# Padding rows sent one behind each of eight loads per queue, and a POOL wait for the copies of one tile only

## The chip, the cores and the metric

The kernel runs on one core of a Trainium2 chip. The metric is the device time of one execution in microseconds (us), lower is better. The engines are PE (TensorE), DVE (VectorE), ACT (ScalarE), POOL (GpSimd) and SP (SyncE); each works through its own list of instructions in order, and they wait for one another through semaphores (counters). SP and POOL issue DMAs here.

## What is computed

An attention layer (with batch normalisation of q, k and v), a layer norm, and then a mixture of eight experts of which every token uses the best two, followed by a second layer norm. There are 32 x 256 = 8192 tokens of 128 numbers, and an expert has 512 hidden units. The part that matters here, cut from the reference:

```python
        logits = _ln(xf, router_ln_scale, router_ln_bias) @ router_w.T + router_b
        probs = jax.nn.softmax(logits, axis=-1)
        topw, topi = jax.lax.top_k(probs, K)
        topw = topw / jnp.sum(topw, axis=-1, keepdims=True)
        gates = jnp.zeros((T, E), xf.dtype).at[jnp.arange(T)[:, None], topi].set(topw)

        def expert(ls, lb, W1, B1, W2, B2):
            h = jax.nn.gelu(_ln(xf, ls, lb) @ W1.T + B1, approximate=False)
            return h @ W2.T + B2
        ys = jax.vmap(expert)(expert_ln_scale, expert_ln_bias, w1, b1, w2, b2)
        out = jnp.einsum('te,etd->td', gates, ys)
    x = _layernorm(x + _L0_attn_ref(x, ...), axis=-1)
    x = _layernorm(x + _L0_ffn_ref(x, ...), axis=-1)
```

## The kernel before

**Stages.** After the set-up, 32 batches go through the attention (up to about 143 us). For each batch POOL scatters its tokens' rows by their first choice of expert into queue1, a table in device memory in which each expert has a region of its own (`scatter`, L551). Then comes the expert stage, in two passes over tiles of 128 rows. Pass 1 has N1 = 71 tiles, 0 to 70: it loads 128 rows of queue1, runs the first choice's expert on them, and POOL scatters the result by the second choice into queue2. Pass 2 has tiles 71 to 141: it loads 128 rows of queue2, runs the second expert, adds and normalises, and POOL scatters the rows into the output. The first NTILE0 = 29 tiles of a pass are listed early, from the counts of the first 18 batches; the other 42 are listed later, once all rows are counted.

**Padding.** An expert's region ends anywhere, but a tile takes 128 rows. So behind the end of each of the eight regions of either queue 128 padding rows are written: sixteen DMAs, which SP issues (`pad`, L417: the end is read from `ends_i`, then one DMA from SBUF to the queue). DVE writes `ends_i` in `list_second_group` (L1362) and raises `s_pad`; POOL raises `s_pad2` when the rows for the second queue carry their numbers. Tiles 29 to 70 of pass 1 may take in padding rows of queue1, tiles 100 to 141 of pass 2 those of queue2.

**SP's order.** SP issues the load of tile j into slot j % 16 (`load_rows`, L423), which first waits for `s_yo` of that slot: the rows of tile j - 16 have been sent and have landed. Up to here SP does 29 loads, then the sixteen pads, then waits for all of the pads, then loads on. Between the two passes it waits for the sends of the tiles that the next loads need (`rows_written`, L432).

**The loop of a tile.** PE transposes a tile's rows (L847), multiplies by the first weights (L854, eight matmuls in the view, 128 x 128 each) and, one tile later, by the second (L864). DVE normalises the rows (L1406, waits for the load), adds the bias (L1400) and adds the result to the rows (`first_result`, L1428, raises `s_ac`). In pass 2 DVE ends a tile with `finish` (L1452), which waits for POOL's root.

**POOL's order.** In pass 1 one turn is `carry(j + 2)`, two small operations on one column of 128 numbers (L568, L569) that put a tile's numbers into its outgoing rows, and `send_on(j)` (L572), the scatter of tile j (L577). `send_on` waits for `s_ac` and, by `pg.settle()` without an argument, until every copy that POOL has issued so far is complete, those of tile j + 2 too. `settle(at)` waits for a count of its own copies (L54). In pass 2 a turn is `root(j)` (L584) and `send_out(j - 1)` (L590).

Of the kernel before, what the change touches and what calls it, by code (L numbers as in the profile page):

```python
# [58 lines left out]
def wait(eng, sem, value):  # L59

    if isinstance(value, int) and value <= 0:
        return
    eng.wait_ge(sem, value)
# [25 lines left out]
def build(nc, x, x_t, wide, low, r_b, w1_t, b1_rows, w2_t, b2, out):  # L89
    NB, T, C = x.shape  # L90
    _, E, H = w1_t.shape
    R = low.shape[0]
    HC = H // P
# [9 lines left out]
    NTILE0 = NB0 * TPB - (E - 1)  # L103

    N1 = NT + E - 1
# [24 lines left out]
    with ExitStack() as ctx:  # L130
# [3 lines left out]
        def sem(name):  # L134
            return ctx.enter_context(nc.semaphore(name))
# [127 lines left out]
        def fold_bank(e):  # L263
# [63 lines left out]
        s_n0, s_tot, s_tabp, s_tabt, s_tab, s_pad, s_zero, s_n0t = [sem(n) for n in (  # L327
            "s_n0", "s_tot", "s_tabp", "s_tabt", "s_tab", "s_pad", "s_zero", "s_n0t")]
        s_rows, s_pad2 = [sem(n) for n in ("s_rows", "s_pad2")]
# [13 lines left out]
        s_padd = sem("s_padd")  # L343
# [28 lines left out]
        def own_wait(eng, s_own):  # L372


            eng.sem_inc(s_own, 1)
# [15 lines left out]
        @block.sync  # L391
        def _(sp):

            def load_chunk(c):
                sp.dma_start(x_all[:, c * CH:(c + 1) * CH, DATA:DATA + P], x_chunks[c]).then_inc(s_x[c], 16)

            def load_columns(c):
                here = slice(c * XT_B * T, (c + 1) * XT_B * T)
                sp.dma_start(xT[:, here], x_t[:, here]).then_inc(s_xt[c], 16)

            for c in range(NCH):
                load_chunk(c)
            for e in range(E):
                sp.dma_start(w1r[:, e], w1_t[:, e]).then_inc(s_w1[e // 3], 16)
                if e + 1 in (W1_FIRST, E - 2):
                    load_columns(int(e >= W1_FIRST))
            for c in range(2, NB // XT_B):
                load_columns(c)
            for e in range(E):
                sp.dma_start(w2T[:, e], w2_t[:, e]).then_inc(s_w2, 16)  # L410
            sp.dma_start(b2_bc[:], b2.rearrange("e d -> (e d)").partition_broadcast(P)).then_inc(s_go, 16)

            sp.wait_ge(s_rows, 1)
            sp.dma_start(queue1[DUMMY:DUMMY + E * P, :].rearrange("(a p) c -> p a c", p=P), pad_rows[:]).then_inc(s_zero, 16)
            sp.dma_start(queue2[DUMMY:DUMMY + E * P, :].rearrange("(a p) c -> p a c", p=P), pad2_rows[:]).then_inc(s_zero, 16)

            def pad(e, second):  # L417
                n = E + e if second else e
                end = sp.value_load(ends_i[0:1, n:n + 1], min_val=e * CAP, max_val=e * CAP + NTOK)
                rows = (pad2_rows if second else pad_rows)[:, e, :]  # L420
                sp.dma_start((queue2 if second else queue1)[bass.ds(end, P), :], rows).then_inc(s_padd, 16)

            def load_rows(j):  # L423
                slot = j % XR
                wait(sp, s_yo[slot], j // XR * 16)
                row = sp.value_load(tab_row[0:1, j:j + 1], min_val=0, max_val=DUMMY + (E - 1) * P)
                if j < N1:
                    sp.dma_start(xg[:, slot, 0:W1], queue1[bass.ds(row, P), :]).then_inc(s_xg[slot], 16)
                else:
                    sp.dma_start(xg[:, slot, :], queue2[bass.ds(row, P), :]).then_inc(s_xg[slot], 16)  # L430

            def rows_written(n_tiles):  # L432

                for j in range(n_tiles - XR, n_tiles):
                    sp.wait_ge(s_yo[j % XR], 16 * (j // XR + 1))

            sp.wait_ge(s_scat[0], SCAT * NB0)
            sp.wait_ge(s_tab, 1)
            for j in range(NTILE0):
                load_rows(j)  # L440
            sp.wait_ge(s_pad, 1)
            sp.wait_ge(s_pad2, 1)
            for second in (False, True):
                for e in range(E):
                    pad(e, second)
            sp.wait_ge(s_scat[1], SCAT * (NB - NB0))
            sp.wait_ge(s_padd, 16 * 2 * E)
            sp.wait_ge(s_tab, 2)
            for j in range(NTILE0, N1):
                load_rows(j)  # L450
            rows_written(N_UP)
            for j in range(N1, N1 + NTILE0):
                load_rows(j)
            rows_written(N1)
            for j in range(N1 + NTILE0, NTILE):
                load_rows(j)
            rows_written(NTILE)
# [3 lines left out]
        def _(pool):  # L461
            pg = Progress(pool, s_pool)
# [88 lines left out]
            def scatter(b):  # L551
# [5 lines left out]
                for t in range(TPB):  # L557
# [3 lines left out]
                        out=queue1, out_offset=bass.IndirectOffsetOnAxis(x_int[:, b * TPB + t, POS1:POS1 + 1], 0),  # L561
                        in_=x_all[:, b * TPB + t, DATA:DATA + W1], in_offset=None).then_inc(s_scat[b >= NB0], 16)

            def carry(j):
                slot = j % XR
                pool.wait_ge(s_gm, j + 1)
                sd = xg[:, slot, ROOT0 - DATA:ROOT0 - DATA + 1]
                pg.did(pool.tensor_tensor(orow[:, slot, SQ0:SQ0 + 1], sd, sd, ALU.mult))  # L568
                pg.did(pool.tensor_copy(orow_int[:, slot, TOK2:TOK2 + 1],  # L569
                                        xg_int[:, slot, TOK - DATA:TOK - DATA + 1]))  # L570

            def send_on(j):  # L572
                slot = j % XR
                pool.wait_ge(s_ac, j + 1)
                pg.settle()
                own_wait(pool, s_own_pool)
                pool.indirect_dma_start(  # L577
                    out=queue2, out_offset=bass.IndirectOffsetOnAxis(xg_int[:, slot, POS2 - DATA:POS2 - DATA + 1], 0),
                    in_=orow[:, slot, :], in_offset=None).then_inc(s_yo[slot], 16)
# [18 lines left out]
            for j in range(CARRY_AHEAD):  # L598
                carry(j)
            for j in range(N1):  # L600
                if j + CARRY_AHEAD < N1:
                    carry(j + CARRY_AHEAD)
                send_on(j)
# [939 lines left out]
```

## Time and profile before

| what | value |
|---|---|
| median of 3 runs | 466.83 us (465.84 to 467.15) |
| profiled execution, its time | 464.84 us |
| its span, first to last instruction | 463.0 us |
| PE busy | 414.6 us, 90% |
| ACT busy | 323.5 us, 70% |
| POOL busy | 321.0 us, 69% |
| DVE busy | 285.0 us, 62% |
| mean granted TensorE clock | 0.949 |

Times in the trace are us from the start of the span. The shares are means over stages with different limits, so a stage is read from its own waits and from the pace of its tiles. A matmul's end is modelled; starts are good for pacing. In a timeline a row is a start, a length, the engine, the line and the operation, and in brackets the idle time of the engine ahead of it with what ended that. SPq is SP's own list of instructions. A clock of 1.00 is 2.4 GHz and 0.50 is 1.2 GHz.

### The profile page before, as it was taken

The page shows a single profiled execution, that of the slowest core. Times are in us where ns is not written, and L with a number is a line of the kernel's source. Part 1 is how long each engine was busy: PE and PEld are TensorE (multiplying, and loading weights), DVE is VectorE, ACT ScalarE, POOL GpSimd, SP SyncE. Part 2 cuts the span into 40 slices and gives each one's busy share as a digit, 9 for nine tenths or more (in the row PEclk, how much of TensorE's full clock was granted, in tenths as well). Part 3 has the DMA queues.
Part 4 walks back from the last instruction along what each step waited for, and adds up shares of the span by engine and source line. Part 5 has one row for each costly group of instructions (what it writes and reads, how often), then busy time and mean ns, then how long its engine had stood idle before and what let it go on. Part 6 is the DMA issues. An engine that isn't in the chain of part 4 may idle for free. (4 is left out here: it accounts for less than half of the span.)

```text
span 463.0 us, 14354 instructions
## 1 busy us (share of the span) xinstructions
PE 414.6 (90%) x3464; PEld 395.7 (85%) x3468; DVE 285.0 (62%) x1612; ACT 323.5 (70%) x826; POOL 321.0 (69%) x538
## 2 busy tenths in 40 slices
PE   8989899999985999960999999995999999999970
PEld 7967788999875989960999999994999999999970
DVE  2455967999996575520555555532666667666662
ACT  2137688999886677850688788883788888887830
POOL 7000577999899866666656656566888888688885
PEclk9999999999995899995899999998899999999995
DMA  9999211111124123344443333444333333333210
GB/s 233 332 405 334 61 36 38 44 45 44 38 69 107 44 60 90 100 130 146 120 118 96 90 89 90 120 121 133 104 107 104 105 106 104 100 94 105 71 36 28
DMA packets 45057, 50.90 MB, mean 110 GB/s; under 512 B 6562, under 2 KB 37026, under 8 KB 44978
## 3 DMA queue, kind: packets, MB, share of 16 engines
q1 hardware_dynamic: 36880, 30.67, 24.7%
q0 software_dynamic: 7728, 18.51, 11.9%
q10 hardware_dynamic: 370, 0.80, 0.6%
q8 instruction: 33, 0.54, 0.5%
q14 instruction: 46, 0.38, 0.3%
HBM read 28.23 MB, written 21.72 MB: 108 GB/s over the span
## 5 line engine op out<-in xcount | busy, mean ns | idle before, releaser
L864 PE MATMUL bank<-w2T,xT 128*128 x1136 | 153.5, 279 | 6.2 <-DVE yt L1400 6.2
L854 PE MATMUL bank<-xT 128*128 128x128 f32 x1136 | 155.3, 281 | 2.1 <-issue 2.1
L864 PEld LDWEIGHTS bank<-w2T,xT 128*128 128x128 f32 x1136 | 141.4, 196 | 6.6 <-issue 6.6
L854 PEld LDWEIGHTS bank<-xT 128*128 128x128 f32 x1136 | 142.4, 197 | 2.4 <-issue 2.4
L886 ACT ACTIVATE xT<-w1T,zero_col 128x512 f32 x142 | 102.4, 722 | 42.3 <-issue 39.6
L577 POOL DMA_INDIRECT queue<-xT,xg x71 | 71.4, 1006 | 57.8 <-POOL xT L569 34.7
L1400 DVE TENSOR_TENSOR yt<-bank,b_bc 128x128 f32<-128x128 f32 x142 | 41.4, 291 | 94.4 <-PE bank L864 66.3
L590 POOL DMA_INDIRECT out<-xT,xg x71 | 75.3, 1061 | 17.1 <-issue 17.1
L1007 ACT ACTIVATE xT<-bank 128x512 f32<-128x512 f32 x142 | 82.2, 579 | 4.3 <-PE bank L854 3.5
L886 ACT ACTIVATE xT<-bank,one_col 128x128 f32<-128x128 f32 x142 | 52.1, 367 | 34.6 <-PE bank L847 29.1
L560 POOL DMA_INDIRECT queue<-x_all x64 | 62.3, 973 | 11.5 <-issue 6.9
L544 POOL MEMSET idle<- 128x512 f32 x64 | 34.5, 538 | 27.3 <-ACT x_all L982 26.7
L584 POOL TENSOR_TENSOR r_z<-ve_z,neg_half 128x1 f32<-128x1 f32 x71 | 42.0, 592 | 4.6 <-DVE ve_z L1447 0.5
L1406 DVE TENSOR_SCALAR xT<-xg 128x128 f32<-128x128 f32 x71 | 26.9, 379 | 17.4 <-DMA xg<-queue 17.1
L847 PE MATMUL bank<-ident,xT 128*128 128x128 f32 x71 | 20.7, 291 | 18.5 <-issue 15.1
L1452 DVE TENSOR_SCALAR xT<-zt,mv_z,r_z 128x128 f32<-128x128 f32 x71 | 26.7, 377 | 16.9 <-POOL r_z L584 16.9
L847 PEld LDWEIGHTS bank<-ident,xT 128*128 128x128 f32 x71 | 10.4, 147 | 19.7 <-issue 18.4
L1428 DVE SCALAR_TENSOR_TENSOR xT<-yt,xg 128x128 f32<-128x128 f32 x71 | 25.1, 354 | 0.1
L1434 DVE SCALAR_TENSOR_TENSOR zt<-yt,xg 128x128 f32<-128x128 f32 x71 | 23.9, 336 | 0.0
L713 PE MATMUL bank<-wvvT,xT 128*128 128x144 f32 x128 | 21.1, 288 | 0.0
L1220 DVE SCALAR_TENSOR_TENSOR x_all<-bank,rinv,x_all 128x136 f32<-128x136 f32 x62 | 19.3, 352 | 1.7 <-issue 0.5
L1439 DVE BATCH_NORM_STATS2 st_z<-zt 128x6 f32<-128x128 f32 x71 | 20.1, 283 | 0.0
(232 smaller groups left out, 726.9 us busy)
## 6 DMA issues: line engine op xcount, KB each, us to landing
xg<-queue SPq DMA_DIRECT2D x71, 129.5 KB
xg<-queue SPq DMA_DIRECT2D x71, 67.5 KB
x_all<-x SPq DMA_DIRECT2D x16, 256.0 KB, 6.1
xT<-x_t SPq DMA_DIRECT2D x8, 512.0 KB, 10.4
w1r<-w_t SPq DMA_DIRECT2D x8, 256.0 KB, 6.4
w2T<-w_t SPq DMA_DIRECT2D x8, 256.0 KB, 11.3
queue<-xT,xg POOLq DMA_INDIRECT x71
out<-xT,xg POOLq DMA_INDIRECT x71
```

Of the source, the lines that this page charges most:

```text
L544: pg.did(pool.memset(idle[:, 0:4, :], 0.0))
L560: pool.indirect_dma_start(out=queue1, out_offset=bass.IndirectOffsetOnAxis(x_int[:, b * TPB + t, POS1:POS1 + 1], 0), in_=x_all[:, b * TPB ...
L577: pool.indirect_dma_start(out=queue2, out_offset=bass.IndirectOffsetOnAxis(xg_int[:, slot, POS2 - DATA:POS2 - DATA + 1], 0), in_=orow[:, s ...
L584: pool.tensor_tensor(r_z[:, at], ve_z[:, at], neg_half[:, 0:1], ALU.pow).then_inc(s_pw, 1)
L590: pool.indirect_dma_start(out=out, out_offset=bass.IndirectOffsetOnAxis(xg_int[:, slot, TOK2:TOK2 + 1], 0), in_=orow[:, slot, 0:P], in_off ...
L847: tr(bank[q % 2][:, 0:P], (orow if k < N1 else xg)[:, slot, 0:P], ident[:]).then_inc(s_gt, 1)
L854: last = mm(bank[2 + s][:, h * P:(h + 1) * P], w1c[:, (q - 1) % WR, h * P:(h + 1) * P], xgT[:, s, :], start=True, stop=True)
L864: last = mm(bank[4 + s][:, 0:P], hs[:, s, h, :], w2T[:, bass.ds(e, 1), h, :].rearrange("p a d -> p (a d)"), start=(h == 0), stop=(h == HC ...
L886: return act.activation(out_, in_, ACT.Identity, bias=bias)
L1007: act.activation(hs[:, s].rearrange("p h t -> p (h t)"), bank[2 + s][:], ACT.Gelu).then_inc(s_hs, 1)
L1400: v.tensor_tensor(yt[:, j % 2, :], bank[4 + j % 2][:, 0:P], b2_bc[:, bass.ds(e * P, P)], ALU.add).then_inc(s_ys, 1)
L1406: v.tensor_scalar(orow[:, slot, 0:P], xg[:, slot, 0:P], xg[:, slot, MEAN - DATA:MEAN - DATA + 1], xg[:, slot, ROOT - DATA:ROOT - DATA + 1] ...
```

## The change

SP no longer issues the sixteen pads in a row behind load 28. It issues a pad of queue1 behind each of the loads 21 to 28, and a pad of queue2 behind each of the loads 63 to 70. Each of the first eight waits for `s_pad` and `s_pad2`, which are counters that stay up once raised. Ahead of load 29 SP waits for the eight pads of queue1 alone, and ahead of load 100 for all sixteen. POOL notes in `carried[j]` how many of its copies had been issued when `carry(j)` was done, and `send_on(j)` waits for that many.

```diff
             for j in range(NTILE0):
                 load_rows(j)
-            sp.wait_ge(s_pad, 1)
-            sp.wait_ge(s_pad2, 1)
-            for second in (False, True):
-                for e in range(E):
-                    pad(e, second)
+                if j >= NTILE0 - E:
+                    sp.wait_ge(s_pad, 1)
+                    sp.wait_ge(s_pad2, 1)
+                    pad(j - (NTILE0 - E), False)
             sp.wait_ge(s_scat[1], SCAT * (NB - NB0))
-            sp.wait_ge(s_padd, 16 * 2 * E)
+            sp.wait_ge(s_padd, 16 * E)
             sp.wait_ge(s_tab, 2)
             for j in range(NTILE0, N1):
                 load_rows(j)
+                if j >= N1 - E:
+                    pad(j - (N1 - E), True)
             rows_written(N_UP)
             for j in range(N1, N1 + NTILE0):
                 load_rows(j)
             rows_written(N1)
+            sp.wait_ge(s_padd, 16 * 2 * E)
             for j in range(N1 + NTILE0, NTILE):
                 load_rows(j)
...
+            carried = {}
+
             def carry(j):
...
                 pg.did(pool.tensor_copy(orow_int[:, slot, TOK2:TOK2 + 1],
                                         xg_int[:, slot, TOK - DATA:TOK - DATA + 1]))
+                carried[j] = pg.n
 
             def send_on(j):
                 slot = j % XR
                 pool.wait_ge(s_ac, j + 1)
-                pg.settle()
+                pg.settle(carried[j])
```

On SP, around the loads of tiles 22 and 23 (they wait for `s_yo6` and `s_yo7`), this stands in a row before:

```order
L426 TENSOR_LOAD tab [waits s_yo6]
L426 ISA x2
L428 ISA
L428 DMA xg<-queue 128x135
L426 TENSOR_LOAD tab [waits s_yo7]
L426 ISA x2
L428 ISA
L428 DMA xg<-queue 128x135
```

And in the changed kernel, from the load of tile 22 to that of tile 23:

```order
L426 TENSOR_LOAD tab [waits s_yo6]
L426 ISA x2
L428 ISA
L428 DMA xg<-queue 128x135
L419 TENSOR_LOAD ends_i [waits s_pad2,s_pad]
L419 ISA x2
L421 ISA
L421 DMA queue<-pad_rows 128x135
L426 TENSOR_LOAD tab [waits s_yo7]
```

A pad with its register load has moved in between the two loads.

On SP, at the load of tile 29, the first of the second list, before (the last of the sixteen pads goes to queue2, 259 numbers a row):

```order
L419 TENSOR_LOAD ends_i
L419 ISA x2
L421 ISA
L421 DMA queue<-pad_rows 128x259
L426 TENSOR_LOAD tab [waits s_tab,s_yo13,s_padd,s_scat1]
L426 ISA x2
L428 ISA
L428 DMA xg<-queue 128x135
```

In the changed kernel, from the load of tile 28 (`s_yo12`) to that of tile 29:

```order
L426 TENSOR_LOAD tab [waits s_yo12]
L426 ISA x2
L428 ISA
L428 DMA xg<-queue 128x135
L419 TENSOR_LOAD ends_i [waits s_pad2,s_pad]
L419 ISA x2
L421 ISA
L421 DMA queue<-pad_rows 128x135
L426 TENSOR_LOAD tab [waits s_tab,s_yo13,s_padd,s_scat1]
```

Of the sixteen pads one is left ahead of this load; the wait for `s_padd` stays, for half the count. POOL's instructions stand in the same order in both kernels; only the count that the send waits for differs.

## Rows read from the trace of the kernel before

**Rows 1.** The page: span, and busy time by engine.

```profile
span 463.0 us, 14354 instructions
PE 414.6 (90%) x3464; PEld 395.7 (85%) x3468; DVE 285.0 (62%) x1612; ACT 323.5 (70%) x826; POOL 321.0 (69%) x538
```

**Rows 2.** The waits: in total us, times, longest us.

```profile
DVE xT L1406 <- DMA xg<-queue: 17.1, 1, 17.1
...
DVE xT L1452 <- POOL r_z L584: 16.9, 24, 8.0
```

**Rows 3.** Timeline of PE, 200 to 236 us: transposes of tiles 28, 29, 31, 34.

```profile
202.62 0.27 PE L847 MATMUL bank<-ident,xT 128*128 128x128 f32 x1
...
219.29 0.48 PE L847 MATMUL bank<-ident,xT 128*128 128x128 f32 x1 [14.61 <-issue]
...
225.61 0.27 PE L847 MATMUL bank<-ident,xT 128*128 128x128 f32 x1
...
231.29 0.27 PE L847 MATMUL bank<-ident,xT 128*128 128x128 f32 x1
```

**Rows 4.** Timeline of SP's queue, 155 to 235 us (start, length of the group, count).

```profile
169.77 26.56 SPq L428 DMA_DIRECT2D xg<-queue  x13
197.34 16.96 SPq L421 DMA_DIRECT2D queue<-pad_rows  x16
217.00 17.50 SPq L428 DMA_DIRECT2D xg<-queue  x16
```

**Rows 5.** Timeline of DVE: result of tile 24, normalise of 29, result of 70.

```profile
201.35 0.35 DVE L1428 SCALAR_TENSOR_TENSOR xT<-yt,xg 128x128 f32<-128x128 f32 x1
...
218.89 0.35 DVE L1406 TENSOR_SCALAR xT<-xg 128x128 f32<-128x128 f32 x1 [17.11 <-DMA xg<-queue]
...
306.43 0.35 DVE L1428 SCALAR_TENSOR_TENSOR xT<-yt,xg 128x128 f32<-128x128 f32 x1
```

**Rows 6.** Timeline of PE, 312 to 333 us: transposes of tiles 78 and 82.

```profile
315.27 0.27 PE L847 MATMUL bank<-ident,xg 128*128 128x128 f32 x1
...
331.03 0.27 PE L847 MATMUL bank<-ident,xg 128*128 128x128 f32 x1
```

**Rows 7.** Timeline of DVE, 319 to 325 us: the first finish of pass 2.

```profile
320.74 0.35 DVE L1452 TENSOR_SCALAR xT<-zt,mv_z,r_z 128x128 f32<-128x128 f32 x1 [7.98 <-POOL r_z L584]
```

**Rows 8.** Timeline of POOL, 312 to 324 us: last two sends, first root.

```profile
317.86 0.96 POOL L577 DMA_INDIRECT queue<-xT,xg  x1 [0.30 <-issue]
319.13 0.96 POOL L577 DMA_INDIRECT queue<-xT,xg  x1 [0.30 <-issue]
320.11 0.59 POOL L584 TENSOR_TENSOR r_z<-ve_z,neg_half 128x1 f32<-128x1 f32 x1
```

**Rows 9.** Timeline of POOL, 206 to 211 us: one turn of pass 1.

```profile
205.90 1.00 POOL L577 DMA_INDIRECT queue<-xT,xg  x1 [0.81 <-POOL xT L569]
206.93 0.21 POOL L568 TENSOR_TENSOR xT<-xg 128x1 f32<-128x1 f32 x1
207.06 0.19 POOL L569 COPY xT<-xg 128x1 int32<-128x1 int32 x1
208.06 1.00 POOL L577 DMA_INDIRECT queue<-xT,xg  x1 [0.81 <-POOL xT L569]
```

**Rows 10.** Timeline of POOL, 165 to 171 us: the first send.

```profile
166.25 1.02 POOL L577 DMA_INDIRECT queue<-xT,xg  x1 [0.81 <-POOL xT L569]
```

**Rows 11.** Timeline of POOL, 120 to 130 us: a memset and a scatter.

```profile
120.59 0.54 POOL L544 MEMSET idle<- 128x512 f32 x1
121.29 0.96 POOL L560 DMA_INDIRECT queue<-x_all  x1 [0.17 <-POOL idle L544]
```

**Rows 12.** Timeline of DVE, 163 to 172 us: the step ahead of `s_pad`.

```profile
165.17 0.18 DVE L1370 TENSOR_SCALAR reach<-start 128x18 f32<-128x18 f32 x1
```

**Rows 13.** Windows: busy us of PE, PEld, DVE, ACT, POOL; granted clock, DMA share, GB/s.

```profile
218.00:224.00 6.00, 4.71 (x22) 4.71 (x23) 3.31 (x18) 2.05 (x4) 3.53 (x8) 0.50 0.46 126
225.00:235.00 10.00, 10.00 (x91) 10.00 (x91) 5.58 (x30) 7.65 (x15) 6.18 (x13) 1.00 0.47 127
```

## Prediction

> **What bounds the kernel now.** I read the totals by engine first, then the list of who waited for whom, then the timelines of PE, SP, POOL and DVE around the two long waits. TensorE is busy for 414.6 of 463.0 us [rows 1], and once the expert stage runs, one tile takes it 1.89 us ((231.29 - 225.61)/3, tiles 31 to 34 [rows 3]). Two places break this pace, and the waits name them: DVE waits once, 17.1 us, for a load of rows, and DVE's last step of a tile waits for POOL, 8.0 us at the longest [rows 2].
>
> The **first hole** is at tile 29, the first of the second list. PE begins tile 28 at 202.62, tile 29 at 219.29 and tile 34 at 231.29 [rows 3]. Six tiles took 28.67 us where 6 x 1.895 = 11.37 would do: 17.3 us lost. SP's queue shows why [rows 4]: load 28 had gone by 196.33, then sixteen pads left from 197.34 to 214.30, 1.06 us each, and after a wait for them to land the loads went on at 217.00. DVE had been ready for tile 29 at 201.78 (218.89 less its 17.11 of idle) and had it at 218.89, 1.9 us after its load was issued [rows 5].
>
> The **second hole** is at the seam of the passes. PE begins tile 78 at 315.27 and tile 82 at 331.03, 15.76 us for four tiles instead of 7.58: 8.2 us lost [rows 6]. Here DVE stands for 7.98 us before its first finish of pass 2 [rows 7], which waits for POOL's first root at 320.11, and POOL was sending pass 1's last tiles until then (317.86, 319.13) [rows 8]. POOL is late because of its own pace. A turn of it is a send of 1.00, two small copies, and 0.81 us of idle that ends with its own copy, 2.16 us from 205.90 to 208.06 [rows 9]. From the first send at 166.25 [rows 10] to the last at 319.13 it made 71 sends, 2.18 us apart in the mean, also while PE stood. Its result for tile 24 was ready at 201.35 [rows 5], but 24 x 2.18 puts that send near 218.6. So pass 1 is **bound by POOL from end to end**: PE, faster by 0.28 us a tile, runs ahead, loses its lead in the first hole, gains it again and stands at the seam.
>
> **Part 1, POOL's wait.** Before, the send of tile j waits for the copies of tile j+2, issued just ahead of it; now for those of tile j, two turns old. No instruction is added or moved. What remains of the 0.81 us gap is bounded by three rows. A send whose wait was met long ago starts 0.30 us after the one before [rows 8]; the scatter of the first stage, behind a memset that it doesn't wait for, starts 0.17 us after it [rows 11]; if the gap were the preparation of a send behind a copy, 0.81 would stay. I take 0.30, from the same instruction with the same operands. A turn is then 1.00 + 0.03 + 0.13 + 0.19 + 0.30 = 1.65 us, which is under PE's 1.89. Send j starts at 166.25 + 1.65j, and its result is there at 201.35 + 1.895(j - 24); the two meet at tile 43. From there POOL waits for results, and at the seam it is level with DVE, so the second hole goes: **-8.2 us**. If 0.5 us of gap stayed (a turn of 1.86), tile 70 would go some 8 us behind its result, where it went 12.7 us behind before (319.13 against 306.43 [rows 5, 8]); with the 8.2 us that this cost, 3.5 would stay.
>
> **Part 2, the pads.** The sixteen pads are not fewer; eight now stand between loads 21 to 28, eight between loads 63 to 70. A pair of load and pad costs SP 1.09 + 1.06 = 2.15 us (17.50/16 and 16.96/16 [rows 4]). Load j also waits until the send of j - 16 has landed: load 16 went at 169.77 behind the send that started at 166.25, 3.5 us later [rows 4, 10]. With the faster POOL, load 21 goes at 169.77 + 5 x 1.65 = 178.0, load 28 seven pairs on at 193.1, its pad ends by 195.2, and the wait for the pads costs what it cost before, 2.7 us (214.30 to 217.00): load 29 goes at 198.0 and its rows can be used at 199.9, where DVE wants them at 201.78. The cover is thin, **1.9 us**; each later load gains 0.8 on that. So the hole goes and its slow restart with it: **-17.3 us**. Were load 29 late, up to 3 us would come back. The new wait for the two flags in front of the first pad holds loads 22 and on; the last step before that flag ran at 165.17 [rows 12], 12 us before SP gets there. The later pads sit in front of loads 64 to 71, which by then have a lead: load 63 goes some 5 us behind tile 47's result (about 245), and DVE uses it near 201.78 + 34 x 1.9 = 266.4, 16 us later; seven pairs lose 7 x 0.26 = 1.8 us of it. Priced at nothing. The third wait for the pads, ahead of load 100, stands behind a wait for all 71 sends, which ends after them.
>
> **The restart.** In 218 to 224 PE had a granted clock of 0.50, so 1.2 GHz, against 1.00 from 225 on [rows 13]. It had stood still for 14.6 us [rows 3], and tiles 29 and 30 took 6.32 us together (219.29 to 225.61) instead of 3.79; those 2.5 us are inside the 17.3. The Trainium skill ("TensorE: Matmul & The Clock Gate", What's actually happening) has the array fall to 1.2 GHz after an idle stretch and return under load. By that, too, the 2.5 us go with the hole; if the low clock came from elsewhere, the sum would be 14.8 + 8.2 = 23.0.
>
> **Why neither part is enough.** Pads alone leave POOL's chain of 71 sends untouched, so the end stays: near 465. POOL's wait alone lets load 28 go at 169.77 + 12 x 1.65 = 189.6, the sixteen pads run to about 207.6 and load 29 goes at 210.3, so the hole shrinks by 6.7 us, and the seam's 8.2 go: near 450. Together: 17.3 + 8.2 = 25.5.
>
> **The sum.** The profiled execution took 464.84 us. 464.84 - 25.5 = 439.3. That execution lay 2.0 us under the median of 466.83, so as a median **441.3 us**. Pass 2 after the seam and the tail keep their length, since POOL runs the same instructions there and PE keeps its pace.
>
> **Rivals.**
> 1. *Most of the gap stays.* A turn of 1.86 us or more, and at worst a load 29 that is late: 3.5 to 10 us come back, 445 to 452. Against it: 0.17 and 0.30 [rows 8, 11]. Chance 0.13.
> 2. *The wait was free.* The 0.81 us is the price of a send behind a copy, whatever it waits for. POOL then makes its 71 sends at 2.18 as before and the seam stays where it is: 466 to 467, no change. For it: every send behind a copy shows it. Against it: the scatter behind a memset doesn't [rows 11]. Chance 0.05. The Trainium skill ("Advanced Engine Details and Errata", Network/Comms) gives 50 to 100 ns for reading a semaphore from a sequencer. An estimate by that page of 0.1 us a turn over 69 turns would give back only 7 us, 460 us; the 0.81 against 0.30 speaks against it, and I give it 0.02 of its own.
> 3. *SP becomes the bound, slower than before.* A pad between two loads could cost SP much more than in a row of pads. With a pair of p us, load 29 is late by 8p - 19.1 (it is early by 1.9 at 2.15), the later group by 8p - 8 x 1.895 - 16 = 8p - 31. Both together pass the 25.5 us gained from p = 4.7 us on; at 5 us the kernel would take 441.3 + 20.9 + 9 = 471. For it: nothing but the thin cover. Against it: loads and pads cost nearly the same each in a row, 1.09 and 1.06 [rows 4]. Chance 0.03.
>
> **How the numbers follow.** Forecast case 0.77 (437 to 445), rivals 0.13, 0.07 and 0.03. The range runs from 437 (a tail without disturbance) to 450, so that it takes in the late load and most of the first rival; about 0.14 is left out. Faster by over 0.3% (1.4 us, about what a measurement of this kernel can tell) is 0.77 + 0.13 + 0.02 = 0.92; the rest of rival 2 is no change, 0.05; rival 3 is slower, 0.03.
>
> **What would show it.** POOL's idle before a send falls from 0.81 to about 0.3 and sends leave 1.65 us apart until tile 43, then 1.9. DVE's 17.1 us wait for rows is gone, SP shows no row of sixteen pads, load 29 goes near 198. The longest wait of DVE's finish is under 2 us, POOL's last send of pass 1 starts near 290, and PE begins tile 71 near 285. The granted clock doesn't fall between 160 and 420. A gap of 0.81, a hole at tile 29 of over 3 us or a stall at the seam would make it wrong.

## The result, and the profile after

The changed kernel took **447.09 us** in the median of 4 runs (445.98 to 447.85), beside 466.99 us for the kernel before, measured along with it; the ratio is 0.9574 (95% interval 0.9546 to 0.9603). The forecast was 441.3 us with a range of 437 to 450. So sign and range held, and 5.8 us of the forecast gain are missing. The same kernel was measured three more times later on and took 440.12, 447.58 and 446.67 us; most of this document is about those 7 us. A run more than 1.5% above the fastest of its kernel counts as slow; only one kernel here had such runs (two of four, in the section on closer scatters).

The page of the changed kernel, span and busy time by engine, answers to [rows 1]:

```profile
span 445.4 us, 14366 instructions
PE 413.4 (93%) x3468; PEld 392.8 (88%) x3468; DVE 284.3 (64%) x1612; ACT 323.2 (73%) x826; POOL 322.0 (72%) x538
```

The work is the same, the span is 17.6 us shorter. The waits of the changed kernel (in total us, times, longest us) answer to [rows 2]:

```profile
DVE yt L1405 <- remote: 8.5, 3, 3.5
DVE xT L1457 <- POOL r_z L589: 8.9, 23, 1.5
```

DVE's wait of 17.1 us for a load of rows is not in the list any more, and its longest wait for a root of POOL is 1.5 us instead of 8.0. What is new is a wait of DVE marked "remote", which is what the view calls one whose releaser it can't find.

**POOL.** One turn of pass 1 in the timeline of POOL of the changed kernel answers to [rows 9]:

```profile
176.41 1.00 POOL L582 DMA_INDIRECT queue<-xT,xg  x1 [0.16 <-issue]
177.45 0.20 POOL L572 TENSOR_TENSOR xT<-xg 128x1 f32<-128x1 f32 x1
177.58 0.19 POOL L573 COPY xT<-xg 128x1 int32<-128x1 int32 x1
177.93 1.01 POOL L582 DMA_INDIRECT queue<-xT,xg  x1 [0.17 <-issue]
```

The gap ahead of a send fell from 0.81 to 0.17 us, a turn from 2.16 to 1.52 us.

**The seam.** The same timeline at the end of pass 1 answers to [rows 8]:

```profile
298.15 0.96 POOL L582 DMA_INDIRECT queue<-xT,xg  x1 [0.93 <-issue]
301.66 0.58 POOL L589 TENSOR_TENSOR r_z<-ve_z,neg_half 128x1 f32<-128x1 f32 x1 [2.55 <-DVE ve_z L1452]
```

POOL, which DVE waited for at 320.74 before [rows 7], now waits for DVE, 2.55 us. The second hole is gone.

**SP.** The timeline of its queue answers to [rows 4]; L421 is a pad, L428 a load:

```profile
170.47 9.74 SPq L428 DMA_DIRECT2D xg<-queue  x6
181.04 0.52 SPq L421 DMA_DIRECT2D queue<-pad_rows  x1
...
197.79 0.33 SPq L428 DMA_DIRECT2D xg<-queue  x1
199.26 0.04 SPq L421 DMA_DIRECT2D queue<-pad_rows  x1
201.60 32.50 SPq L428 DMA_DIRECT2D xg<-queue  x23
```

There is no row of sixteen pads, and load 29 goes at 201.60 instead of 217.00.

**Where the missing time is.** PE's transposes, set beside those of the kernel before, give the balance. Tile 10 begins at 165.44 (before: 165.96), 0.5 us early. Tiles 10 to 28 take 43.96 us (before: 36.66), 7.3 us more. Tiles 28 to 70 take 81.2 us, where the 97.5 of before less the hole's 17.3, so 80.2, was counted on, 1.0 us more. Tiles 70 to 141 take 135.6 us (before: 143.7, less the seam's 8.2), and the tail is 19.2 us in both. That makes 7.9 us over the forecast span of 463.0 - 25.5 = 437.5, and 445.4 was measured. The forecast had added 2.0 us since the profiled execution of before was below its median; that of the changed kernel (447.26 us) is not, so between the medians 5.8 us are left.

The 7.3 us lie between 173 and 190 us, ahead of the old hole. PE's timeline there (transposes of tiles 15, 16 and 17, L852, and the second product, L869), then ACT's (copies of the transposed tiles 15 and 16) and DVE's (bias of tiles 12 and 13):

```profile
178.15 0.30 PE L852 MATMUL bank<-ident,xT 128*128 128x128 f32 x1
...
180.11 1.15 PE L869 MATMUL bank<-w2T,xT 128*128 x8 [0.71 <-ACT xT L1012]
181.36 0.30 PE L852 MATMUL bank<-ident,xT 128*128 128x128 f32 x1
...
186.54 0.42 PE L852 MATMUL bank<-ident,xT 128*128 128x128 f32 x1
```

```profile
181.63 0.37 ACT L891 ACTIVATE xT<-bank,one_col 128x128 f32<-128x128 f32 x1 [1.66 <-remote]
...
185.47 0.37 ACT L891 ACTIVATE xT<-bank,one_col 128x128 f32<-128x128 f32 x1 [0.94 <-remote]
```

```profile
181.01 0.29 DVE L1405 TENSOR_TENSOR yt<-bank,b_bc 128x128 f32<-128x128 f32 x1 [2.96 <-remote]
...
185.54 0.29 DVE L1405 TENSOR_TENSOR yt<-bank,b_bc 128x128 f32<-128x128 f32 x1 [3.46 <-remote]
```

PE transposes tile 15 at 178.15, and ACT, which stands idle, copies it at 181.63, 3.5 us later; for tile 16 it is 4.1 us (181.36 and 185.47). In the steady pace, in this kernel and in the one before, this distance is **0.31 us**. The kernel before at tile 15:

```profile
177.93 0.27 PE L847 MATMUL bank<-ident,xT 128*128 128x128 f32 x1
178.24 0.37 ACT L886 ACTIVATE xT<-bank,one_col 128x128 f32<-128x128 f32 x1
```

DVE gets the products of PE late in the same way. The view names no other engine that is waited for. So either PE's signals reach ACT and DVE late, or PE finishes later than its modelled ends say; the trace can't tell these apart, and both are called **the delay** from here on. It begins at tile 13, whose copy at 174.74 comes 1.08 us behind its transpose, and ends when POOL has caught up with the results (tile 13, sent at 187.07) and its sends no longer leave 1.52 us apart. It comes back once, smaller: POOL has a pause ahead of 257.92, makes three sends 1.52 us apart (257.92, 259.44, 260.96), ACT copies tiles 55 and 56 1.6 and 1.7 us behind their transposes, and PE's tile 57 comes 3.16 us behind tile 56 instead of 1.90.

### The profile page after: what moved, and what is told of

The parts are those of the page before. It is cut to its first block, busy times and chain, and to the rows that moved or that the text cites. A ratio compares the mean times of both kernels' runs of the same rounds, so it can differ in the third digit from the quotient of the medians.

```text
span 445.4 us, 14366 instructions
## 1 busy us (share of the span) xinstructions
PE 413.4 (93%) x3468; PEld 392.8 (88%) x3468; DVE 284.3 (64%) x1612; ACT 323.2 (73%) x826; POOL 322.0 (72%) x538
## 4 chain that ended last, share of the span: by engine, by line
PE 68%; DVE 10%; issue 9%; POOL 7%; ACT 2%; DMA 1%; another core or an unknown queue 0%; POOLq 0%; ACTq 0%; SPq 0%; DVEq 0%
PE bank L859 23%; PE bank L869 23%; POOL r_z L589 4%; PE bank L664 4%; PE bank L852 3%; POOL out L595 2%; PE bank L718 2%; PE bank L704 2%; DVE x_all L1225 2%; PE bank L655 2%; DMA x_all<-x 1%; PE bank L739 1%; PE bank L727 1%; PE bank L748 1%; DVE nmax L1147 1%
## 5 line engine op out<-in xcount | busy, mean ns | idle before, releaser
L869 PE MATMUL bank<-w2T,xT 128*128 x1136 | 151.6, 277 | 4.3 <-issue 2.3
L859 PE MATMUL bank<-xT 128*128 128x128 f32 x1136 | 153.2, 278 | 2.1 <-ACT xT L891 1.7
L869 PEld LDWEIGHTS bank<-w2T,xT 128*128 128x128 f32 x1136 | 139.0, 193 | 5.5 <-issue 5.5
L859 PEld LDWEIGHTS bank<-xT 128*128 128x128 f32 x1136 | 140.0, 194 | 2.7 <-ACT xT L891 2.0
L595 POOL DMA_INDIRECT out<-xT,xg x71 | 75.1, 1058 | 17.1 <-issue 17.1
L852 PE MATMUL bank<-ident,xT 128*128 128x128 f32 x71 | 20.4, 287 | 4.4 <-DVE xT L1411 3.7
L891 ACT ACTIVATE prT<-bank 128x384 f32<-128x384 f32 x32 | 15.7, 489 | 5.4 <-PE bank L739 3.6
```

Source lines behind the costliest of these rows:

```text
L595: pool.indirect_dma_start(out=out, out_offset=bass.IndirectOffsetOnAxis(xg_int[:, slot, TOK2:TOK2 + 1], 0), in_=orow[:, slot, 0:P], in_off ...
L852: tr(bank[q % 2][:, 0:P], (orow if k < N1 else xg)[:, slot, 0:P], ident[:]).then_inc(s_gt, 1)
L859: last = mm(bank[2 + s][:, h * P:(h + 1) * P], w1c[:, (q - 1) % WR, h * P:(h + 1) * P], xgT[:, s, :], start=True, stop=True)
L869: last = mm(bank[4 + s][:, 0:P], hs[:, s, h, :], w2T[:, bass.ds(e, 1), h, :].rearrange("p a d -> p (a d)"), start=(h == 0), stop=(h == HC ...
L891: return act.activation(out_, in_, ACT.Identity, bias=bias)
```

## The experiments

### Each part alone

**Pads alone.** POOL's wait as before:

```diff
-                pg.settle(carried[j])
+                pg.settle()
```

> The pads as in the changed kernel, POOL's wait as before. The changed kernel spends 7.3 us more than forecast between tiles 10 and 28 of pass 1, where ACT and DVE stand waiting for PE (ACT's copy of a transposed tile starts up to 4.1 us behind the transpose instead of 0.31 us). Theory A: POOL's sends at 1.52 us apart delay PE's signals for as long as they come so fast. Theory B: the pads between the loads do it. Prediction's step: POOL's 71 sends at 2.18 us bound pass 1, so pads alone give nothing, 464 to 467 us, with the last send of pass 1 near 319 and a stall at the seam. A: the copy stays 0.31 us behind the transpose at tiles 13 to 20. B: it is 1 to 4 us behind at tiles 13 to 20, and the time is still near 466 because POOL hides it.

It took 465.25 us (10 runs), ratio 0.9963 (0.9936 to 0.9989). The hole at tile 29 is filled: PE begins it 2.15 us behind tile 28. All of it comes back further on, as the waits of this kernel show:

```profile
DVE xT L1411 <- DMA xg<-queue: 29.7, 33, 2.3
DVE xT L1457 <- POOL r_z L589: 21.9, 24, 13.2
```

The wait at the seam has grown from 8.0 to 13.2 us, and 33 short waits for loads appear, since a load waits for the send sixteen tiles back. The last send of pass 1 starts at 321.83. The copy stays 0.31 to 0.34 us behind the transpose at tiles 14 to 20, with the pads between the loads and sends 2.16 us apart or more: against B, and what A expects.

**The wait alone.** The sixteen pads in a row as before, and of the change this:

```diff
+                carried[j] = pg.n
...
-                pg.settle()
+                pg.settle(carried[j])
```

> POOL's wait as in the changed kernel, the sixteen pads in a row as before. The prediction had 450 us: the hole at tile 29 shrinks by 6.7 us, the seam's stall goes. A: the delay at tiles 13 to 17 is here as in the changed kernel, so DVE wants tile 29 some 7 us later and the hole is only 1 to 4 us; 448 to 451 us. B: no delay at tiles 13 to 17, a hole of 8 to 10 us at tile 29; 449 to 452 us. The times lie close, the trace tells them apart.

It took 449.0 us, ratio 0.963 (0.960 to 0.966); the forecast had 450. SP's queue and the wait for tile 29:

```profile
168.64 18.97 SPq L428 DMA_DIRECT2D xg<-queue  x13
188.45 17.48 SPq L421 DMA_DIRECT2D queue<-pad_rows  x16
208.58 26.20 SPq L428 DMA_DIRECT2D xg<-queue  x22
```

```profile
DVE xT L1409 <- DMA xg<-queue: 9.4, 1, 9.4
```

The hole shrank from 17.1 to 9.4 us of DVE's wait, and the seam's stall is gone (1.6 us at most). Both parts of the change and their sum behave as the prediction had them. The delay is **not** there, though the sends leave 1.52 us apart: the copies of tiles 13 to 20 start 0.31 to 0.36 us behind the transposes. That spoke against theory A, on this chip.

### Spacing the sends, pacing the loads

**Spaced.** The changed kernel with a memset of 128 columns in each turn of POOL:

```diff
                 carried[j] = pg.n
+                pg.settle(carried.get("space"))
+                pg.did(pool.memset(idle[:].rearrange("p a c -> p (a c)")[:, 0:128], 0.0))
+                carried["space"] = pg.n
```

> The changed kernel with one memset of 128 columns on POOL in each turn of pass 1 (0.2 us of work with no use but to space the sends), so sends leave about 1.74 us apart while POOL catches up. A: the delay at tiles 10 to 28 shrinks or goes, and the time is 440 to 444 us; POOL is level with DVE near tile 57. B: the delay stays and the time is 447 us. If the delay goes but 1.74 us is too slow to be level at the seam, up to 2 us come back there.

439.81 us, ratio 0.9431 (0.9396 to 0.9465). Sends leave 1.67 to 1.77 us apart, and there is no delay. Load 29 leaves at 201.31 here and DVE waits 3.0 us for its rows, so the cover of that load is used up; the kernel is as fast all the same.

**Loads paced.** A load among 16 to 28 also waits for a result:

```diff
             for j in range(NTILE0):
+                if j >= XR:
+                    sp.wait_ge(s_ac, j - 8)
                 load_rows(j)
```

> The changed kernel, but the load of tile j (16 to 28) also waits until the result of tile j - 9 is there, so that loads leave at the pace of results, 1.9 us apart, while POOL's sends stay 1.52 us apart. A: the delay stays, about 447 us. C, a third theory, that the closer stream of loads does it: the delay goes, 439 to 442 us.

440.5 us, ratio 0.9459 (0.9417 to 0.9501), no delay either, with sends 1.52 us apart. Two remedies with nothing in common had the same effect, and the kernel with the wait alone needed none. All four ran on one chip, and the first measurement of the changed kernel had not run beside them. So it had to be measured again.

### The same kernel again

> The changed kernel, unaltered, once more. In its first profile PE's results reached ACT and DVE late between tiles 10 and 18 (up to 4.1 us instead of 0.31 us behind the transpose), 7.3 us in all. The kernel with POOL's wait alone runs the same instructions until 178 us, with sends 1.52 us apart, and shows nothing of this, so theory A (sends too close) has fallen. Theory D: the delay belongs to the program (the pads between the loads meet the fast sends) and comes back on every chip: 445 to 448 us. Theory E: it is an accident of timing in the first measurement, of a chip or of a moment: 438 to 442 us, with the copy 0.31 us behind the transpose at tiles 13 to 20.

**440.12 us** (6 runs, 438.74 to 441.27), ratio 0.9411 (0.9382 to 0.9439), on chip 2, where the four above had run as well. No delay, sends 1.52 us apart, POOL level with the results at tile 25. By itself this says theory E. PE's transpose and ACT's copy of tile 15 here:

```profile
180.05 0.27 PE L852 MATMUL bank<-ident,xT 128*128 128x128 f32 x1
180.36 0.37 ACT L891 ACTIVATE xT<-bank,one_col 128x128 f32<-128x128 f32 x1
```

It also gives the forecast's sum a clean reading: 1.2 us under 441.3. Its profiled execution reaches tile 10 at 168.03, 2.1 us later than before, in a part that the change doesn't touch; from there every stretch is within 0.3 us of the forecast (10 to 28: 36.9, 28 to 70: 80.0 for 80.2, 70 to 141: 135.5).

**Pads early.** The eight pads of the first queue between loads 15 and 16:

```diff
-                if j >= NTILE0 - E:
+                if j == XR - 1:
                     sp.wait_ge(s_pad, 1)
                     sp.wait_ge(s_pad2, 1)
-                    pad(j - (NTILE0 - E), False)
+                    for e in range(E):
+                        pad(e, False)
```

> The changed kernel, but the eight pads of the first queue stand between load 15 and load 16, where SP waits for POOL's first send anyway. D: without pads between loads 21 and 28 there is no delay at tiles 13 to 18, 438 to 441 us. E: the same as the changed kernel run beside it, within 1 us. In either case load 16 may be late by up to 1 us (the pads run from about 166 to 174.5), which shows at tile 16, not later.

438.71 us, ratio 0.9395 (0.9358 to 0.9432); the same as the changed kernel beside it within the intervals.

> The kernel with a memset of 128 columns in each of POOL's turns, unaltered, beside the changed kernel on one chip. D: 7 us faster than the changed kernel, near 440 us. E: within 1 us of it, both near 440 us.

440.94 us, ratio 0.9444 (0.9409 to 0.9479). Where the delay is absent, spacing the sends gains nothing; its median is 0.8 us higher, within the intervals.

### Is there such an effect at all? Closer scatters

**Scatters close.** The changed kernel without the memset that stands ahead of every scatter of the attention stage:

```diff
                 pg.settle()
-                pg.did(pool.memset(idle[:, 0:4, :], 0.0))
```

> The changed kernel without the memset of 0.54 us between two scatters of the attention stage, so that a batch's two scatters leave about 1.1 us apart instead of 1.67 us. Theory F: close indirect DMAs of POOL can delay what PE tells ACT and DVE, and the first profile of the changed kernel (sends 1.52 us apart between 167 and 188 us) was a case of it. F: between 80 and 143 us PE, ACT and DVE show waits for one another that the changed kernel doesn't have, and the expert stage begins 2 us or more later. E (that delay was an accident of one measurement, nothing to do with the pitch): the attention stage takes the same time within 0.5 us, since POOL was not its bound, 439 to 441 us.

> The changed kernel a third time, unaltered. E: 438 to 442 us as in its second measurement; if it comes out near 447 us again, both speeds belong to the kernel and the profile shows the delay between tiles 10 and 18 again.

Both ran on chip 12. The changed kernel took 447.58 us (ratio 0.9598, 0.9569 to 0.9627), so both of its speeds are real. Without the memset the four runs took 462.98, 469.62, 473.67 and 474.71 us (median 471.64). They scatter widely, so no exact price can be given and the comparison with the kernel before (466.47 us) is unclear. Against the changed kernel it is clear: the fastest is 14.2 us above the slowest of the changed kernel (448.81), and the mean of the lower two, 466.3, is 18.7 us above its median. That came from taking 0.54 us of idle work at a time away from an engine that no other waits for between 60 and 143 us. POOL's timeline of the kernel without the memset:

```profile
100.38 0.96 POOL L561 DMA_INDIRECT queue<-x_all  x1 [1.01 <-issue]
101.64 0.96 POOL L561 DMA_INDIRECT queue<-x_all  x1 [0.30 <-issue]
```

A batch's two scatters leave 1.26 us apart (1.1 was expected) instead of 1.67 us. The window from 100 to 140 us (busy us and instructions of PE, PEld, DVE, ACT and POOL, granted clock, DMA share, GB/s), of the changed kernel and then of the one without the memset, both on chip 12:

```profile
100.00:140.00 40.00, 38.73 (x333) 34.35 (x330) 38.72 (x289) 35.66 (x153) 35.67 (x50) 1.00 0.17 51
```

```profile
100.00:140.00 40.00, 37.10 (x298) 32.98 (x296) 35.04 (x258) 30.40 (x133) 22.25 (x25) 0.96 0.13 41
```

PE got through 298 matmuls instead of 333, with less DMA traffic, and the waits of this kernel have the mark of the delay again, now for another product of PE:

```profile
ACT prT L890 <- remote: 15.0, 5, 3.7
```

The first tile of the expert stage begins at 164.38 instead of 144.66, 19.7 us late. In this profiled execution (462.98 us, beside 448.81) 14.2 us of it reach the end, since the expert stage has less of the delay: tiles 10 to 28 take 37.8 us instead of 44.0. So an accident of one measurement (E) is out, and F is borne out on chip 12: with POOL's scatters closer behind one another, ACT gets PE's products late. This kernel was not run on another chip.

### The remedy where the delay is

> The changed kernel a fourth time, as the reference of this call. So far it took 447.1 us, 440.1 us (chip 2) and 447.6 us (chip 12). If it takes 446 to 449 us here, this chip shows the delay between tiles 10 and 18 and the two kernels beside it tell whether spacing the sends removes it; if it takes 438 to 441 us, this chip doesn't show it and they can only tell that spacing costs nothing.

> The changed kernel with a memset of 128 columns in each turn of POOL, sends 1.68 to 1.75 us apart instead of 1.52. Theory F (close indirect DMAs delay what PE tells ACT and DVE, on some chips): where the reference takes 447 us this takes 439 to 443 us, and ACT's copy stays 0.31 us behind the transpose at tiles 12 to 17. If 1.7 us is still too close, 444 to 447 us. Where the reference takes 440 us, the same within 1 us.

> The same memset, and the eight pads of the first queue between load 15 and load 16. F: 438 to 441 us on either kind of chip, since neither close sends nor pads behind the loads 21 to 28 are left. If the pads between the loads had a part in the delay of the reference, this is faster than the kernel with the memset alone by more than 2 us where the reference is slow.

The three ran on chip 9. The changed kernel took 446.67 us (ratio 0.9579, 0.9530 to 0.9627), with the memset 439.62 us (0.9445, 0.9395 to 0.9494), with the memset and early pads 439.01 us (0.9405, 0.9357 to 0.9454). The copy of tile 15 in ACT's timeline of the changed kernel on this chip, whose transpose began at 179.08, and in that of the spaced kernel, whose transpose began at 176.26:

```profile
183.96 0.37 ACT L891 ACTIVATE xT<-bank,one_col 128x128 f32<-128x128 f32 x1 [0.96 <-remote]
```

```profile
176.57 0.37 ACT L894 ACTIVATE xT<-bank,one_col 128x128 f32<-128x128 f32 x1
```

4.88 us against 0.31 us. POOL's timelines of the two, at the same place:

```profile
177.20 1.01 POOL L582 DMA_INDIRECT queue<-xT,xg  x1 [0.17 <-issue]
...
178.73 1.01 POOL L582 DMA_INDIRECT queue<-xT,xg  x1 [0.16 <-issue]
```

```profile
176.37 1.01 POOL L585 DMA_INDIRECT queue<-xT,xg  x1 [0.17 <-POOL idle L577]
...
178.06 1.02 POOL L585 DMA_INDIRECT queue<-xT,xg  x1 [0.17 <-POOL idle L577]
```

The sends are 1.53 us apart in one and 1.69 us in the other, and nothing else in the program was changed: 0.2 us of useless work a turn gives back 7.0 us. The later small delay is gone too (tile 57 comes 1.90 us behind tile 56).

**Loads and pads as rivals.** A load waits for a send, so the memset spaces the loads as well. And whether the pads between the loads add to the delay can't be told by the third kernel, where the sends are spaced already; it differs from the second by 0.6 us, within the intervals. The traces tell more. SP's queue of the changed kernel on chip 12, then that of the third kernel (spaced, pads early) on chip 9:

```profile
170.53 9.62 SPq L428 DMA_DIRECT2D xg<-queue  x6
180.98 0.36 SPq L421 DMA_DIRECT2D queue<-pad_rows  x1
```

```profile
176.34 17.23 SPq L428 DMA_DIRECT2D xg<-queue  x13
```

On chip 12 tile 13 is transposed at 175.11 and copied at 180.16, 5.05 us later, and the first pad leaves only at 180.98; in the first measurement and on chip 9 too the delay is there before the first pad. So the pads don't start it. In the third kernel thirteen loads leave within 17.2 us, closer than the six of the changed kernel on chip 12, and tiles 13 to 17 are copied 0.51 us behind their transposes at most. So closer loads alone don't make it either. That fast sends and loads are needed together in the expert stage is not excluded.

| changed kernel | chip | us | delay at tiles 13 to 17 |
|---|---|---|---|
| first measurement | not recorded | 447.09 | up to 4.1 us |
| second | 2 | 440.12 | none |
| third | 12 | 447.58 | up to 5.6 us |
| fourth | 9 | 446.67 | up to 4.9 us |

## Why the prediction was right or wrong

**What bounded the kernel: right.** Pass 1 was POOL's from end to end. The pads alone (465.25 us, near 465 forecast) and the wait alone (449.0, near 450) are the two numbers that the prediction gave for the halves, and both halves are needed.

**The gap: right in kind, mis-sized.** 0.30 us was taken, 0.17 measured. The better row was the scatter behind a memset [rows 11], not the send behind a send [rows 8]. POOL is level with the results at tile 25 in the second measurement, not at 43. The Trainium skill ("Advanced Engine Details and Errata", Network/Comms) gives 50 to 100 ns for reading a semaphore from a sequencer. The prediction's estimate by it, 0.1 us a turn, is not borne out as the price of this wait: the gap fell by 0.64 us.

**The seam, -8.2 us: right.** Tiles 70 to 141 took 135.6 us in place of 143.7.

**The pads, -17.3 us: right, with its cover used up.** Load 29 was to go at 198.0. In the second measurement, which runs 2.1 us later at tile 10 (168.03 against 165.96), it goes at 201.89, so at 199.8 by the clock of before, 1.8 us behind the forecast and just inside the cover of 1.9:

```profile
204.28 0.35 DVE L1411 TENSOR_SCALAR xT<-xg 128x128 f32<-128x128 f32 x1 [0.21 <-DMA xg<-queue]
```

DVE waits 0.21 us for it. What was off was the pair of load and pad: load to load it took 2.3 to 2.7 us there (181.26, 183.56, 186.27, 188.96, 191.24, 193.64, 195.91, 198.26), not 2.15, the sum of two prices that each came from a row of equals. Over seven pairs that is 1.9 us, load 21 was 1.2 us late by itself, and 1.3 us came back behind load 28, where 4.9 us were counted on until load 29 and 3.6 passed. The pads of the second queue cost nothing, as priced: tiles 28 to 70 ran at 1.903 us each in that measurement.

**The restart and the clock: right where the delay is absent.** In the second measurement the granted clock is 1.00 in every stretch from 165 to 420, as forecast. In the first measurement the granted clock dipped once in pass 1, in the delay itself (0.70 in 185 to 190), and not at tile 29.

**The sum: right where nothing else happens, 5 to 6 us too low elsewhere.** 441.3 was forecast; 440.1 on chip 2. On the three other measurements it was about 447, above the forecast case (437 to 445). That 447 still lies in the range is luck: its upper part was kept for a late load and for a longer turn of POOL, and neither happened. The step that failed is the one that ends "From there POOL waits for results, and at the seam it is level with DVE", taken as a pure gain. What the runs show in its place is the delay at tiles 13 to 17, 7.3 us, and the small one at tiles 55 and 56. The prediction looked at what a faster POOL frees and at the loads that it triggers, and never at what POOL's own closer DMAs do to the rest. None of the rivals held it. The kernel had a sign of it: a function named `part_transfers` puts a memset without a use ahead of every scatter, and the rows quoted for the gap [rows 11] are that very memset. It was read as a price and not as a question: what is it there for?

**What stays open.** Which resource the delay comes from isn't shown. The DMA share was 0.36 to 0.48 in the delay (175 to 190 us) and 0.49 behind it without one (195 to 200), and in the kernel with close scatters it was lower than in the one beside it, so it isn't traffic as such. Why chip 2 doesn't show it at 1.52 us is open as well (closer scatters were not tried there), and so is where between 1.53 and 1.67 us it sets in on chip 9. That pacing the loads, or dropping the early pads, would also help where the delay is was not tried; those kernels ran on chip 2.

## What to carry to other kernels

When an engine that issues indirect DMAs gets faster, look at how close its DMAs now leave, and at whether other engines' products arrive later while they do; a little idle work that spaces them can be worth far more than it costs (7.0 us for 71 memsets of 0.2 us, on chip 9). Where one engine's chain runs beneath two holes, they have to be closed together: each half alone gave 1.7 and 17.9 us, both gave 26.9 us where the delay was absent. And where the runs of one measurement agree within 2.6 us but measurements of the same kernel differ by 7 us, compare only what ran side by side.

## What the runs showed of the hardware

- With indirect DMAs of POOL 1.52 us apart (128 rows of 259 numbers), ACT copied PE's transposed tiles up to 5.6 us behind the transpose instead of 0.31 us on chip 12 and up to 4.9 us on chip 9, and not late at all on chip 2. At 1.67 us apart or more no run showed it; on chip 9 this gave back 7.0 us.
- With scatters of 135 numbers a row 1.26 us apart in pairs instead of 1.67 us, the attention stage ended 19.7 us later in the profiled execution on chip 12.
- A wait of POOL for its own last copy ahead of a DMA costs 0.64 us (a gap of 0.81 against 0.17), for a copy of one column.
- A load and a pad in turn take SP 2.3 to 2.7 us, while in a row of its own kind each takes 1.06 to 1.09 us.
